# New in-order schedules for all engines of an attention stage: later reciprocals, scalings and squares, q and k projected a whole unit ahead, every transfer of squares issued by SyncE

## The reference

```
qkv = einsum('bse,ehd->bshd', xn, w_qkv)        # 16 heads, head size 64; q, k, v = split
probs = softmax(where(tril, q k^T / 8, -large)) # 1024 x 1024 for each batch and head
attn = einsum('bshd,hde->bse', probs v, w_out)
out = x + attn + moe(xn)                        # 8 experts, top 2, capacity 2048 tokens each
```

## Time and profile before

| what | value |
|---|---|
| median of three runs | 3291.39 us |
| profiled execution, its own time | 3287.48 us |
| span of the profiled execution | 3285.6 us |
| mean granted TensorE clock | 0.964 |
| TensorE (PE) busy | 2915.4 us, 89% |
| VectorE (DVE) busy | 2120.5 us, 65% |
| GpSimd (POOL) busy | 1740.3 us, 53% |
| ScalarE (ACT) busy | 1702.1 us, 52% |

### The profile page before, as it was taken

The page is one execution under the profiler, slowest core; times in us unless marked ns, Lnnn a source line. Parts: engine busy times, 40 slices in busy tenths (PEclk is TensorE's granted clock), DMA queues, the critical chain, the costliest instruction groups (busy, mean ns, idle before and its releaser), DMA issues.

```text
span 3285.6 us, 61637 instructions
## 1 busy us (share of the span) xinstructions
PE 2915.4 (89%) x21321; PEld 2329.7 (71%) x21321; DVE 2120.5 (65%) x4640; ACT 1702.1 (52%) x3934; POOL 1740.3 (53%) x2631
## 2 busy tenths in 40 slices
PE   4699999999988888888888888888889888888888
PEld 3589998999966666666666666666666666666665
DVE  7744443444367677766677776777767777777775
ACT  3544444444455555555555554555555555555554
POOL 3212222212056666666566666666666666666664
PEclk8799999999999999999999999999999999999999
DMA  6112222221144555555544644545555455555543
GB/s 231 54 40 78 70 76 70 74 71 49 49 118 116 134 132 138 124 127 141 125 110 110 157 120 112 146 121 125 127 137 129 118 134 140 129 123 149 123 107 90
DMA packets 248777, 371.61 MB, mean 113 GB/s; under 512 B 77392, under 2 KB 177744, under 8 KB 248480
## 3 DMA queue, kind: packets, MB, share of 16 engines
q1 hardware_dynamic: 216000, 276.31, 32.9%
q0 software_dynamic: 32480, 91.44, 10.4%
HBM read 102.80 MB, written 33.55 MB: 42 GB/s over the span
## 4 chain that ended last, share of the span: by engine, by line
PE 18%; POOL 14%; DVE 14%; ACT 11%; issue 10%; DMA 5%; DVEq 0%; ACTq 0%; POOLq 0%
PE O L1257 9%; ACT pr L1287 8%; DVE squares L1392 6%; PE S L1225 6%; POOL pr L1429 5%; DMA yg<-y,sel 5%; POOL pT L1460 3%; DVE pr L1349 2%; DVE res L1375 2%; POOL wl L1441 2%; POOL yg L1473 1%; DVE kls L1383 1%; PE W L1183 1%; DVE ol L1399 1%; POOL yg L1479 1%
## 5 line engine op out<-in xcount | busy, mean ns | idle before, releaser
L1287 ACT ACTIVATE pr<-pr,negm 128x512 f32<-128x512 f32 (+7 forms) x1024 | 786.3, 770 | 839.8 <-DVE negm L1349 839.8
L1429 POOL TENSOR_SCALAR pr<-pr,rinv 128x512 f32<-128x512 f32 (+7 forms) x1024 | 762.0, 750 | 619.4 <-DVE rinv L1355 605.5
L1349 DVE CUSTOM_DVE_ANT_0 pr<-S,late 128x512 f32<-128x512 f32 (+7 forms) x1024 | 715.1, 749 | 108.8 <-PE S L1225 108.8
L1257 PE MATMUL O<-pT,vv 128*64 128x256 f32 (+1 forms) x5120 | 570.7, 376 | 0.0
L1392 DVE STREAM_TRANSPOSE squares<-pr 128x640 f32<-128x640 f32 x504 | 512.3, 1027 | 0.0
L1257 PEld LDWEIGHTS O<-pT,vv 128*64 128x64 f32 x5120 | 359.9, 142 | 196.3 <-issue 47.8
L832 DVE TENSOR_TENSOR hl<-h,hh 128x512 fp32r<-128x512 f32 x256 | 192.2, 751 | 315.8 <-ACT hh L793 315.6
L789 ACT ACTIVATE h<-pH,b1c 128x512 f32<-128x512 f32 x256 | 176.1, 688 | 365.8 <-PE pH L719 337.8
L1183 PE MATMUL W<-ident,pr 128*128 128x128 f32 x1332 | 214.3, 288 | 159.8 <-POOL pr L1429 75.1
L1225 PE MATMUL S<-khf,qh 64*128 64x512 f32 (+2 forms) x1024 | 221.1, 427 | 125.5 <-DVE kls L1383 125.5
L1460 POOL DMA_DIRECT2D pT<-squares x504 | 263.2, 529 | 113.3 <-DVE squares L1392 110.9
(11 more groups left out here) (176 smaller groups left out, 6891.4 us busy)
## 6 DMA issues: line engine op xcount, KB each, us to landing
pT<-squares SPq DMA_DIRECT2D x756, 128.0 KB
pT<-squares SPq DMA_DIRECT2D x756, 96.0 KB, 2.6
pT<-squares POOLq DMA_DIRECT2D x252, 128.0 KB
pT<-squares POOLq DMA_DIRECT2D x252, 96.0 KB, 2.9
y<-yb SPq DMA_DIRECT2D x128, 128.0 KB, 1.7
wr<-in_L_attn_w_qkv SPq DMA_DIRECT2D x128, 128.0 KB, 3.7
x<-in_L_attn_x SPq DMA_DIRECT2D x16, 512.0 KB, 8.8
xn<-xn SPq DMA_DIRECT2D x16, 512.0 KB, 4.4
```

The lines of the kernel that those rows point to most:

```text
L1257: ins = e.matmul(O[hs, o0 + a:o0 + GQ], vv[n // 2 % 2][:, kt, vs], turned_p, start=(kt == 0), stop=(kt == KT - 1))
L1287: e.activation(p, p, ACT.Exp, bias=negm[:, c0:c0 + 1], scale=-1.0, accum_out=rsum[:, c0:c0 + 1]).then_inc(expd.sem, 1)
L1349: e.tensor_tensor_reduce(room_of(n, i, h)[:, off:off + w], S[h][:, off:off + w], late[:, SEQ - w:], 1.0, -MASKED, ALU.add, ALU.min, negm[: ...
L1429: e.tensor_scalar(p, p, rinv[:, c0:c0 + 1], 1.0, ALU.mult, ALU.mult).then_inc(scaled.sem, 1)
```

## The change

The order of work is written anew for every engine; no operation of the arithmetic goes or comes.

- TensorE: p2 and p3 move to steps 16 and 17 and are now for the next unit, as p0 (12) and p1 (10) are; the scores' round 1 waits for p3 of the unit before. t30 and t31 move to step 4, t20 and t21 to 8. Row 1 is turned as `t1` at 13 and row 0 as `t0` at 16. `v0` goes to step 0, `xn` from 18 to step 1, `v1` to 9, o0 to 5, o1 to 9, o2 to 11, o3 to 18. Run 0 moves from step 19 of its unit to step 3 of the next.
- VectorE: one reciprocal instruction for each round, at the start of the next round and ahead of that round's row minima. Both squares of a row stand at the third step of the next round. Pieces are read at steps given by `DVE_STEP`, and ahead of the row minima of their step.
- ScalarE: pieces are read at steps given by `ACT_STEP`.
- GpSimd: all scalings of a round stand at the start of the next, row 0 ahead of row 5. `place_rest` is gone; weight splits and the steps of the gather move; `total` is done in the next unit.
- SyncE issues all 16 transfers of each group. The weight loads stand ahead of `place` of group 3. At a batch's start the stores and refills of groups 0 to 2 follow `place` of group 3, and store and refill of group 3 stay at the end of SyncE's unit.

```diff
+    SCALE_ORDER = [(i, h) for rows in ROUNDS for i in (rows if 0 not in rows else rows[::-1]) for h in range(2)]
...
-             "t10": [(1, 0, 0, 2), (0, 0, 0, 1)], "t11": [(1, 1, 0, 2), (0, 1, 0, 1)]}
+             "t1": [(1, 0, 0, 2), (1, 1, 0, 2)], "t0": [(0, 0, 0, 1), (0, 1, 0, 1)]}
...
-    STEP_OF = {"p2": 0, "p3": 1, "o0": 2,
-               "o1": 4, "v0": 5,
-               "t30": 8, "t31": 8, "o2": 9, "t20": 10, "t21": 10,
-               "v1": 12, "p0": 13, "t10": 14, "t11": 14,
-               "p1": 16, "o3": 17, "xn": 18}
-    BANK_OF = {"p2": 0, "p3": 1, "o0": 2,
-               "o1": 0, "v0": 1,
-               "t30": 2, "t31": 0, "o2": 1, "t20": 2, "t21": 0,
-               "v1": 1, "p0": 2, "t10": 0, "t11": 1,
-               "p1": 0, "o3": 2, "xn": 1}
+    STEP_OF = {"v0": 0, "xn": 1,
+               "t30": 4, "t31": 4, "o0": 5,
+               "t20": 8, "t21": 8, "o1": 9, "v1": 9, "p1": 10, "o2": 11,
+               "p0": 12, "t1": 13,
+               "t0": 16, "p2": 16, "p3": 17, "o3": 18}
+    ACT_STEP = {"v0": 2, "xn": 2, "t30": 4, "t31": 4, "t20": 8, "t21": 8, "v1": 10, "p1": 12,
+                "p0": 12, "t1": 13, "t0": 16, "p2": 17, "p3": 18}
+    DVE_STEP = {"xn": 3, "o0": 6, "o1": 10, "p1": 12, "o2": 12, "p0": 15, "p2": 19, "p3": 19, "o3": STEPS + 2}
...
+    DVE_STEP |= {f"t6{h}{c}": 2 for h in range(2) for c in range(2)}
...
-    BEFORE = ["p0", "p1", "v0", "v1"]
+    BEFORE = ["p0", "p1", "p2", "p3", "v0", "v1"]
...
-    RUN_STEP = [(0, 19), (1, 7), (1, 15)]
+    RUN_STEP = [(1, 3), (1, 7), (1, 15)]
...
-    POOL_AT = {"choose": 1, "place3_0": 4, "place3_1": 5, "split_w": 6, "fetch0": 8, "fetch1": 9, "weigh": 11, "add": 12,
-               "split_wv": 14, "place2_0": 16, "place2_1": 17, "total": 19}
+    POOL_AT = {"split_w": 1, "total": 5, "choose": 6, "fetch0": 8, "fetch1": 9, "weigh": 13, "add": 14, "split_wv": 17}
...
-        recip = Count(sem("s_recip"), QT)
+        recip = Count(sem("s_recip"), len(ROUNDS))
         squared = Count(sem("s_squared"), 2 * len(SQUARED))
-        placed = {g: Count(sem(f"s_placed{g}"), 16 * QUARTERS * (QUARTERS - 1)) for g in (2, 3)}
-        pool_placed = {g: Count(sem(f"s_pool_placed{g}"), 16 * QUARTERS) for g in (2, 3)}
+        placed = {g: Count(sem(f"s_placed{g}"), 16 * QUARTERS * QUARTERS) for g in (2, 3)}
...
+        def read_at(n, s, step):
+
+            return [(m, p) for m in (n - 1, n) if 0 <= m <= UNITS for at, p in pieces(m) if step.get(p, at + 1) == s + (n - m) * STEPS]
...
-                for a in range(QUARTERS - 1):
+                for a in range(QUARTERS):
...
+                if n + 2 < UNITS:
+                    e.wait_ge(wlo.sem, wlo.at(n, MC))
+                    load_w(n + 2)
                 if n > 0:
                     place(n - 1, 3)
                 if b > 0 and u == 0:
-                    store(b - 1, 0)
-                    store(b - 1, 1)
-                    refill(b, 0)
-                    refill(b, 1)
-                if n + 2 < UNITS:
-                    e.wait_ge(wlo.sem, wlo.at(n, MC))
-                    load_w(n + 2)
-                if b > 0 and u == 0:
-                    store(b - 1, 2)
-                    refill(b, 2)
+                    for g in range(3):
+                        store(b - 1, g)
+                    for g in range(3):
+                        refill(b, g)
                 if n < UNITS - 1:
...
-                unit = n + (f == 0)
+                unit = n + 1
...
-                    e.wait_ge(dve.sem, dve.at(n - 1, "p1"))
+                    e.wait_ge(dve.sem, dve.at(n - 1, "p0"))
+                    if n == 0:
+                        e.wait_ge(dve.sem, dve.at(n - 1, "p1"))
                 if r == 1:
-                    e.wait_ge(dve.sem, dve.at(n, "p3"))
+                    e.wait_ge(dve.sem, dve.at(n - 1, "p3"))
...
-            def reciprocals(n, i):
-                c0 = column(n, i, 0)
-                e.wait_ge(expd.sem, expd.at(n, PLACE[i, 1] + 1))
-                e.reciprocal(rinv[:, c0:c0 + 2], rsum[:, c0:c0 + 2]).then_inc(recip.sem, 1)
+            def reciprocals(n, r):
+                c0, c1 = column(n, ROUNDS[r][0], 0), column(n, ROUNDS[r][-1], 1) + 1
+                e.wait_ge(expd.sem, expd.at(n, FIRST[r + 1]))
+                e.reciprocal(rinv[:, c0:c1], rsum[:, c0:c1]).then_inc(recip.sem, 1)
...
-            for n, s in ALL + END:
+            for n, s in ALL + END + [(UNITS + 1, s) for s in range(SUB)]:
                 r, x = s // SUB, s % SUB
+                m, q = back(n, s, SUB)[0], (r - 1) % len(ROUNDS)
+                if x == 0 and 0 <= m < UNITS:
+                    reciprocals(m, q)
                 if run_at(*back(n, s, 1)):
                     run(*run_at(*back(n, s, 1)))
+                for of, name in read_at(n, s, DVE_STEP):
+                    if by_dve(name):
+                        work(of, name)
                 if n < UNITS and x < len(ROUNDS[r]):
                     for h in range(2):
                         row_min(n, FIRST[r] + 2 * x + h)
                 if (n, s) == (0, 2):
                     e.wait_ge(s_wohi, 1)
                     e.tensor_tensor(wol[:], wo_raw, woh[:].bitcast(F32), ALU.subtract).then_inc(s_wolo, 1)
-                if n < UNITS and 2 <= x < 2 + len(ROUNDS[r]):
-                    reciprocals(n, ROUNDS[r][x - 2])
-                for name in names_at(*back(n, s, 1)):
-                    if by_dve(name):
-                        work(back(n, s, 1)[0], name)
-                m, q = back(n, s, SUB)[0], (r - 1) % len(ROUNDS)
-                if x >= 2 and 0 <= m < UNITS and in_squares(m, ROUNDS[q][0]):
-                    square(m, ROUNDS[q][0], x - 2)
+                if x == 2 and 0 <= m < UNITS and in_squares(m, ROUNDS[q][0]):
+                    for h in range(2):
+                        square(m, ROUNDS[q][0], h)
...
-                e.wait_ge(recip.sem, recip.at(n, j // 2 + 1))
+                e.wait_ge(recip.sem, recip.at(n, ROUND_OF[i] + 1))
...
-            def place_rest(n, g, b):
-
-                if b == 0:
-                    e.wait_ge(squared.sem, squared.at(n, 4 * g - 4))
-                    if n > 0:
-                        e.wait_ge(pv.sem, pv.at(n - 1, RUN_OF[g] + 1))
-                for i in (b, b + 1):
-                    e.dma_start(*strip(g, QUARTERS - 1, i)).then_inc(pool_placed[g].sem, 16)
...
-            for n, s in ALL:
+            for n, s in ALL + END:
                 r, x = s // SUB, s % SUB
                 m, q = back(n, s, SUB)[0], (r - 1) % len(ROUNDS)
-                if x >= 2:
-                    scale(n, FIRST[r] + x - 2)
-                elif m >= 0 and len(ROUNDS[q]) > 1:
-                    scale(m, FIRST[q] + 2 + x)
+                if x == 0 and 0 <= m < UNITS:
+                    for j in range(FIRST[q], FIRST[q + 1]):
+                        scale(m, j)
                 for name, at in POOL_AT.items():
                     if s != at:
+                        continue
+                    if name == "total" and n > 0:
+                        total(n - 1)
+                    if n == UNITS:
                         continue
```

More of the change, by code:

```diff
@@ L894, in attention_and_sum @@
+    DVE_STEP = {"xn": 3, "o0": 6, "o1": 10, "p1": 12, "o2": 12, "p0": 15, "p2": 19, "p3": 19, "o3": STEPS + 2}
+    BANK_OF = {"v0": 0, "xn": 1,
+               "t30": 2, "t31": 0, "o0": 1,
+               "t20": 2, "t21": 0, "o1": 1, "v1": 2, "p1": 0, "o2": 1,
+               "p0": 2, "t1": 0,
+               "t0": 2, "p2": 0, "p3": 1, "o3": 2}
     END_STEP = {4: (UNITS - 1, 12), 5: (UNITS - 1, 16), 6: (UNITS, 0), 7: (UNITS, 4)}
+    DVE_STEP |= {f"t6{h}{c}": 2 for h in range(2) for c in range(2)}
@@ L922, in pieces @@
             return [(0, p) for p in BEFORE]
-        there = {"p0": n + 1 < UNITS, "p1": n + 1 < UNITS, "p2": n < UNITS, "p3": n < UNITS, "v0": n + 1 < UNITS,
-                 "v1": n + 1 < UNITS, "xn": n + AHEAD < TILES}
+        there = {p: n + 1 < UNITS for p in ("p0", "p1", "p2", "p3", "v0", "v1")} | {"xn": n + AHEAD < TILES}
         own = [(s, p) for p, s in STEP_OF.items() if there.get(p, n > 0 if p[0] == "o" else n < UNITS)]
@@ L1130, in project @@
                 W, f, of_k = work_bank(name), int(name[1]) // 2, int(name[1]) % 2
-                unit = n + (f == 0)
+                unit = n + 1
                 t0 = unit // PAIRS % 2 * QT + f * HT
-                if name == "p0" and n >= 0:
+                if name == "p1" and n >= 0:
                     e.wait_ge(wlo.sem, wlo.at(n, MC))
@@ L1178, in turn_p @@
                 i, h, _, _ = TURNS[name][-1]
-                e.wait_ge(scaled.sem, scaled.at(unit, PLACE[i, h] + 1))
+                e.wait_ge(scaled.sem, scaled.at(unit, SCALE_ORDER.index((i, h)) + 1))
                 for i, h, k0, blocks in TURNS[name]:
@@ L1324, in _ @@
                     run(*run_at(*back(n, s, 1)))
-                for name in names_at(*back(n, s, 1)):
+                for m, name in read_at(n, s, ACT_STEP):
```

(17 more changed lines are left out.)

4 lines of the change are left out of this document (removed).

## The result

The changed kernel takes 3215.6 us (median of four runs, 3212.8 to 3221.3) against 3293.8 us before: a ratio of 0.9768, 95% interval 0.9741 to 0.9795. It is 78 us faster. I had forecast 3258 us, 42 us too much. The time lies in my range, but the gain is more than twice the one that I forecast. The profiled execution took 3221.3 us of its own, 66 us less than that of before.

The account below looks back on a forecast made before the run. No engine is full: a ring of in-order queues, TensorE idling 4.4 us a unit plus 1.5 of slow clock. Terms -44, +28, -19 and +2 give -33: 3254.5 us, so 3258 as median; range 3175 to 3335.

Parts of the forecast that it names:

- The main mechanism: TensorE at xn waits for its tile, issued behind 16 transfers on SyncE: 2.9 or 4.1 us, mean 3.5.
- An ordinary unit: Attention unit with xn, not behind a store: 31.1 + 3.5 + 1.3 + 0.2 = 36.1 us against 37.0.
- one behind a store: Unit after a batch's store, six times: tile wait of 8.6 us, the unit costs 41.7 us.
- t30's wait: TensorE behind round 1's scores waits for row 3's scaling: 1.2 us plus 0.3 at t31, 1.5 a unit.
- The placed squares: SyncE's transfers of groups 2 and 3 land before their runs: both hidden, the first by 3 us or more.
- units without xn: Last eight units: t30's wait of 1.5 and 0.7 for clock and small waits, 33.3 us against 35.7: -19.
- the 1.3 us after a gap: Slow TensorE clock behind xn's wait adds 1.3 us a unit, bounds 0 and 1.7.
- The first step: p2 and p3 a unit ahead end TensorE's wait for the low part of k, 2.0 us a unit.
- for GpSimd's issues I count nothing: GpSimd loses eight issues a unit, four taking 2.12 us; it has idle time there, so no gain counted.
- Rival 1: Slower: reciprocals ahead of the next round's minima wait for the last exponential, delaying the scores: 3352 us; chance 0.20.
- Rival 2: Tile there earlier: 1.2 us left of the 3.5 wait, half its clock loss: 3140 us; chance 0.12.
- Rival 3: TensorE's clock stays at 2.4 GHz despite the gaps: 3178 us; chance 0.11.

Follow-up runs that it names:

- run 0: Piece of TensorE's work (2.3 us), not a follow-up kernel; put back at step 19 of its own unit on the kernel with the early tile: 3125.8 us, ratio 0.9501.
- the fastest kernel: Changed kernel with the tile's load ahead of group 2's transfers, v1 ahead of t30 and t31, GpSimd issuing 4 of 16 transfers per group: 2939.1 us, ratio 0.8932.
- the early tile: Changed kernel with the next tile's load issued on SyncE ahead of group 2's 16 transfers instead of behind them: 2985.1 us, ratio 0.9084.

## Why the prediction was right and wrong

**The main mechanism was right in place, and its size near.** The tile's wait was put at 2.9 and 4.1 us in turn and 8.6 behind a store. Measured are 2.6, 4.1 and 7.4. Taking it away gave 231 us. An ordinary unit was put at 36.1 us and took 35.8 ((1853.2 - 6 x 40.4) / 45), one behind a store at 41.7 and took 40.4. t30's wait was put at 1.5 and measured 1.1. The placed squares were hidden, as said, but for one wait of 1.1 us in the stretch of units without xn; once the units grow short they are not (2963 against 2939 us).

**What was mis-sized: the unit terms of the sum.** The sum was -33 us and the profiled executions differ by -66. Each trace is cut at the first product of a unit's scores, into units 1 to 54 and units 55 to 62. The first row is units 1 to 54 of the changed kernel, whose units 55 to 62 are the row of 253.10 us above; then come both stretches of the kernel before:

```profile
947.90:2908.70 1960.80, 1754.55 (x13285) 1346.15 (x13284) 1416.57 (x3079) 1084.07 (x2702) 1073.15 (x1622) 0.93 0.54 131
```

```profile
945.80:2940.70 1994.90, 1756.26 (x13285) 1335.22 (x13284) 1423.77 (x3241) 1072.58 (x2703) 1308.11 (x2054) 0.96 0.52 129
2940.70:3228.10 287.40, 255.63 (x1954) 195.46 (x1952) 208.49 (x474) 156.47 (x392) 191.50 (x300) 0.97 0.52 127
```

By the sum's own terms:

| term | forecast | measured |
|---|---|---|
| ordinary units with xn | 49 x (36.1 - 37.0) = -44 | 48 x (35.80 - 36.94) = -55 |
| six behind a store | 6 x (41.7 - 37.0) = +28 | 6 x (40.40 - 36.95) = +21 |
| units without xn | 8 x (33.3 - 35.7) = -19 | 8 x (31.63 - 35.92) = -34 |
| start and end | +2 | +7.2 (first scores) - 5.2 (unit 0) + 0.0 (unit 63) = +2 |
| sum | -33 | -66 |

SyncE loads 55 tiles, so xn is made for units 0 to 54, and not to 55 as I had written; this moves one unit between two rows and is worth 3 us. The step that failed is the length given to each kind of unit:

- **A unit without xn, 33.3 us, was the largest error.** It was 31.1 of work, 1.5 of wait at t30 and 0.7 for the clock and small waits. Measured are 243.60 / 8 = 30.4 busy at full clock, a wait of 1.0 and 0.1 for the rest: 31.6.
- **A unit behind a store, 41.7 us, took 40.4** (the six that start at 1236.2, 1526.3, 1816.4, 2106.7, 2399.7 and 2690.6 us), mainly because the store's landing held SyncE up for 2.4 us in the unit shown above and not 3.6: the wait was 7.4 us and not 8.6.
- **An ordinary unit, 36.1 us, took 35.8.** It was 31.1 of work, 1.3 of clock, 3.5 of wait and 0.2 of small waits. Measured are a wait of 3.4, no small one, and 32.4 busy, which is the forecast's 31.1 + 1.3. But this agreement is luck. One unit with xn ran at full clock and shows the work alone, 30.6 us, so the slow clock cost 1.8:

```profile
987.40:1020.80 33.40, 30.60 (x247) 24.16 (x246) 26.09 (x58) 19.95 (x51) 20.95 (x32) 1.00 0.54 131
```

So "The work of TensorE at full clock is thus 37.0 - 4.4 - 1.5 = 31.1 us a unit" was 0.5 too much for the changed kernel and the 1.3 us after a gap 0.5 too little. The two errors cancel in the ordinary units and don't in the last ones, which have no such gap. For the kernel before, 31.1 was near: a unit of it at full clock is busy 31.4 us.

```profile
982.30:1018.40 36.10, 31.36 (x250) 23.89 (x248) 26.40 (x61) 19.77 (x50) 25.31 (x41) 1.00 0.51 127
```

Why the same matmuls are busy for 30.6 us after the change isn't settled. PE's busy time holds modelled tails of matmuls, so part of each stop may be booked as work, and the changed kernel has one stop where the kernel before has three or four; but the fastest kernel, with hardly a stop, shows 31.0 us again. Each unit term is a small difference of two numbers near 36, so an error of 1% of a unit is more than a third of the 0.9 us forecast for it. The last 10 us of the miss are the median: I put it 3.9 us above the profiled execution, and it was 5.7 us below.

**The first step was right for the wrong reason.** "p2 and p3 a unit ahead end the first wait" named what that move does alone. Alone it does nothing of use: it also takes p2 and p3 out of round 0, so that TensorE is through with it 2.7 us sooner; it then stands 2.2 us for round 0's minima instead of 2.0 for k, and the kernel got 1% slower. The changed kernel fills that round with v0, xn and run 0; taking run 0 out of it brought 2.1 us of waits back. The same goes for "for GpSimd's issues I count nothing": taken alone that part is a loss of 1.7%, with a longer wait for GpSimd's gather, which I hadn't looked at.

**Rivals.** Rival 1, minima held up by the reciprocals, didn't come about: no matmul of the changed kernel's 51 units waits for negm. With the early tile, reciprocals and scalings in the later round are even worth 144 us, because ScalarE is further when VectorE asks (87.5 us of waits against 271.9). Rival 2, less of the tile's wait, is what sharing the issues brings about, 3053 us. Rival 3, full clock: the mean clock fell, 0.946 against 0.964.

**The clock.** One wait of 2.6 us or more a unit came with a granted clock of 0.93, 5.3 us in six pieces of at most 1.3 with 1.00, waits of 1.9 and 0.4 with 0.96, and waits of 0.8 and 2.4 with 0.99. Spread waits cost least here, but neither their sum nor the longest of them orders the cases. Even units of one kernel with the same waits differ. With the reciprocals in their own round, both of these units have waits of 1.8 to 1.9 and 0.4 us, and the second is 1.2 us shorter:

```profile
1219.00:1253.20 34.20, 31.95 (x247) 25.21 (x246) 26.30 (x60) 20.02 (x51) 23.84 (x38) 0.95 0.61 150
1253.20:1286.20 33.00, 30.73 (x249) 23.99 (x248) 25.89 (x60) 19.89 (x51) 24.28 (x39) 1.00 0.52 133
```

The Trainium skill ("TensorE: Matmul & The Clock Gate", Part 1) says that idleness closes the gate and sustained work opens it; the long waits of the changed kernel agree, but for the unit at 987.4 us, which waited 2.8 us and stayed at 1.00, and the spread ones show that idle time as such need not. What decides between 0.95 and 1.00 at equal waits stays open.

**The transfers.** The 16 issues took 10.03 us where I had 10.5, 0.63 us each. The Trainium skill ("DMA: Bandwidth & Descriptors", Rules for kernel authors) advises to issue a transfer early and to wait for it late. The change moved the wait for one transfer of 128 KB seventeen steps earlier in TensorE's list and left its issue where it was; this case puts the price at 231 us in 3216.

## What to carry to other kernels

When a piece of work is moved earlier in one engine's list, look at the queue that issues its transfer: list what stands ahead of it there, and move the transfer with the piece. When a wait is removed by moving work away, ask what that work was covering: the engine now comes sooner to the next thing it must wait for. In a ring of in-order queues fill each round with enough work of the fullest engine to cover what the others need in it, and put an instruction that waits for another engine behind all that doesn't need it.

## What the runs showed that I had not expected

- Idle time of 5.3 us a unit in six short waits left TensorE's clock at 1.00, while one wait of 3.8 us on the mean came with 0.93, which cost some 1.8 us more. Units of one kernel with equal waits ran at 0.95 and at 1.00.
- Taking eight transfers a unit off GpSimd and giving them to SyncE made GpSimd wait longer for its own gathers, 65.5 against 38.0 us in the same stretch, and the kernel 1.7% slower.
